# Attention in groups of four heads and one query block, with two-bank exponentials and four banks for scores beside two for maxima

## The reference

```python
def attn(h, Wq, bq, Wk, bk, Wv, bv, Wo, bo):           # 16 heads, hd = 16, S = 2048
    q, k, v = (h @ Wq.T + bq), (h @ Wk.T + bk), (h @ Wv.T + bv)   # each reshaped to (B, S, 16, 16)
    scores = jnp.einsum('bqhd,bkhd->bhqk', q, k) / jnp.sqrt(hd)
    scores = jnp.where(causal, scores, finfo.min)
    attn = jax.nn.softmax(scores, axis=-1)
    return jnp.einsum('bhqk,bkhd->bqhd', attn, v).reshape(B, S, H) @ Wo.T + bo
...
x = x + 0.5 * ffn(layernorm(x))
x = x + attn(layernorm(x))
x = x + 0.5 * ffn(layernorm(x))
```

## Time and profile before

| | |
|---|---|
| median of 3 runs | 1116.4 us (1113.87 to 1118.17) |
| the profiled execution | 1118.69 us, its span 1117.0 us |
| TensorE busy | 1071.8 us (96%) |
| VectorE busy | 699.0 us (63%) |
| ScalarE busy | 577.9 us (52%) |
| GpSimd busy | 112.6 us (10%) |
| mean granted TensorE clock | 0.994 of full speed |
| chain that ended last | PE 87%, DVE 6%, ACT 2%, issue 2%, DMA 1% |

### The profile page before, as it was taken

One profiled execution on the slowest core, in us unless ns is written; L12 is line 12 of the kernel. 1 busy time (PEld: TensorE's weight loads), 2 busy tenths in 40 slices (PEclk: granted clock), 3 DMA queues, 4 the chain that ended last, 5 costly groups with the idle time before them and its releaser, 6 DMA issues.

```text
span 1117.0 us, 17563 instructions
## 1 busy us (share of the span) xinstructions
PE 1071.8 (96%) x6448; PEld 707.1 (63%) x6448; DVE 699.0 (63%) x1620; ACT 577.9 (52%) x1107; POOL 112.6 (10%) x409
## 2 busy tenths in 40 slices
PE   4999999998999989999999999999999999999998
PEld 3888888887876533333333333333349888888887
DVE  5986545446556487888888888888544434344333
ACT  4764443342344656666777776777663333333322
POOL 1000000000001136331111111111100000000000
PEclk9999999998999899999999999999999999999999
DMA  6001040060030732322022202200000000000000
GB/s 195 2 1 47 7 126 1 11 175 16 10 123 1 202 65 55 67 53 53 14 41 54 53 1 54 53 1 2 1 1 1 1 20 1 1 19 1 20 1 19
DMA packets 75223, 43.81 MB, mean 39 GB/s; under 512 B 47161, under 2 KB 68993, under 8 KB 75137
## 3 DMA queue, kind: packets, MB, share of 16 engines
q1 hardware_dynamic: 75137, 42.68, 15.7%
HBM read 25.63 MB, written 16.78 MB: 38 GB/s over the span
## 4 chain that ended last, share of the span: by engine, by line
PE 87%; DVE 6%; ACT 2%; issue 2%; DMA 1%; SPq 0%; POOL 0%; ACTq 0%; DVEq 0%; POOLq 0%
PE psum L850 16%; PE psum L635 14%; PE psum L782 12%; PE psum L723 11%; PE psum L738 10%; PE psum L867 8%; PE psum L650 8%; DVE attn_part_max L1327 2%; PE psum L792 2%; PE psum L682 2%; ACT attn_prob L1141 1%; PE psum L826 1%; PE psum L694 1%; PE psum L124 1%; DVE attn_junk L1330 1%
## 5 line engine op out<-in xcount | busy, mean ns | idle before, releaser
L1141 ACT ACTIVATE attn_prob<-psum 128x512 f32<-128x512 f32 (+3 forms) x640 | 301.2, 540 | 145.7 <-PE psum L723 142.0
L1327 DVE TENSOR_REDUCE attn_part_max<-psum 128x1 f32<-128x512 f32 x384 | 243.7, 684 | 50.1 <-PE psum L738 48.2
L635 PE MATMUL psum<-ffn_xt,all_w_hi 128*128 128x512 f32 x512 | 166.0, 406 | 0.0
L782 PE MATMUL psum<-attn_prob,attn_vals 128*32 128x512 f32 (+3 forms) x1280 | 156.9, 544 | 0.1
L1330 DVE CUSTOM_DVE_ANT_0 attn_junk<-psum,attn_mask 128x128 bf16<-128x128 f32 (+3 forms) x256 | 116.9, 485 | 24.9 <-PE psum L738 24.4
L1432 DVE TENSOR_TENSOR ffn_act_out<-ffn_act_out,psum 128x512 f32<-128x512 f32 x64 | 44.0, 688 | 109.3 <-ACT ffn_act_out L1177 109.2
L650 PE MATMUL psum<-all_w_hi,ffn_inner 128*128 128x256 f32 x512 | 105.0, 288 | 0.1
L1177 ACT ACTIVATE ffn_act_out<-psum 128x512 f32<-128x512 f32 x64 | 38.2, 597 | 127.3 <-PE psum L850 127.3
L635 PEld LDWEIGHTS psum<-ffn_xt,all_w_hi 128*128 128x128 f32 x512 | 92.7, 192 | 16.4 <-issue 0.3
L867 PE MATMUL psum<-all_w_hi,ffn_inner 128*128 128x256 f32 x512 | 102.5, 283 | 0.1
L635 PE MATMUL psum<-ffn_xt,all_w_lo 128*128 128x512 f32 x256 | 100.7, 393 | 0.0
(11 more groups left out here) (150 smaller groups left out, 1674.2 us busy)
## 6 DMA issues: line engine op xcount, KB each, us to landing
qk_rows<-qkv_parts SPq DMA_DIRECT2D x16, 384.0 KB, 2.5
qk_rows<-qkv_parts SPq DMA_DIRECT2D x16, 256.0 KB, 2.9
attn_q_early<-qk_rows SPq DMA_DIRECT2D x8, 384.0 KB, 4.5
attn_q_late<-qk_rows SPq DMA_DIRECT2D x8, 384.0 KB, 3.7
attn_k_mid<-qk_rows SPq DMA_DIRECT2D x3, 768.0 KB, 6.7
attn_k_late<-qk_rows SPq DMA_DIRECT2D x3, 768.0 KB, 7.3
all_x<-in_L_attn_h SPq DMA_DIRECT2D x4, 512.0 KB, 6.7
v_rows<-qkv_rows_v SPq DMA_DIRECT2D x16, 128.0 KB, 2.5
```

Source lines behind the costliest of these rows:

```text
L635: last = nc.tensor.matmul(psum[:, 2 * m + q % 2, :], w_part[a][:, 3 * g + m, pl, o:o + P], xt[:, b % 2, c, pl, :], start=(n == 0), stop=(n ...
L782: last = nc.tensor.matmul(psum[r:r + 32, O0, at:BT], vals[:, k0 * SUB + kb + k, 2 * hd:2 * hd + 32], prob[:, (4 * d + 2 * k + hd) % PRING, ...
L1141: nc.scalar.activation(prob[:, n % PRING, at:BT], psum[:, S0 + n % SBANKS, at:BT], ACT.Exp).then_inc(s["exp"], 1)
L1327: nc.vector.tensor_reduce(to, psum[:, bank, :], AX.X, ALU.max).then_inc(s["max_read"], 1)
```

## The change

Groups become one query block and four heads: 16 groups. A step becomes one block of 128 keys and the four heads' scores, so there are again 160 steps of four scores, 640 maxima and four `weigh` matmuls per step.

- Scores get four banks (2 to 5) and their wait stands on j = 0 and j = 2 alone; one exponential reads two banks and writes 1024 elements (two heads). Maxima get two banks (0 and 1).
- `quota(d)` counts chunks of four maxima: 4 in step 9, 2 in steps 10 to 13, 1.25 a step until step 44, then 1. The chunks of a group are ordered with the key block outermost. Chunks also wait for keys and queries that are loaded four steps before them, so steps 66, 67, 94, 95, 122 and 123 hold none and steps 68, 96 and 124 hold three.
- `turn_max(g)`, `copy_max(g)` and `split_max(g)` run once for four heads, `max_row(g)` issues four DMAs instead of two. By the table, groups 3, 9, 11, 13 and 15 are turned in steps 15, 59, 87, 115 and 143, one step before they begin (16, 60, 88, 116, 144); group 2 is turned in 11 and begins in 12.
- `gather` becomes four transposes of 128 columns per group of four heads. It was four matmuls against a matrix `pick` of 34 columns per group of two heads, which also added the two halves of the sums.
- `mask_prob` clears two heads at once. Keys, queries and values are loaded by query block and by key block, into a ring of six.
- Weight turning and the first output projection move forward by one to three steps.

```diff
-KSLOTS = 12
-LOADS = 3
-SBANKS = 3
-MBANKS = 3
+KSLOTS = 6
+NHQ = 4
+SBANKS = 4
+MBANKS = 2
 PRING = 8
-VW = 34
+VW = 67
+VALUES_AT = (0, 2, 33, 35)
...
-            groups = [(qt, p) for half in range(2) for p in range(NPAIR) for qt in (2 * half, 2 * half + 1)]
+            groups = [(qt, u) for half in range(2) for u in range(NH // NHQ) for qt in (2 * half, 2 * half + 1)]
             NG_A = len(groups)
-            steps = [(g, kb) for g, (qt, _) in enumerate(groups) for kb in range(0, SUB * (qt + 1), 2)]
+            steps = [(g, kb) for g, (qt, _) in enumerate(groups) for kb in range(SUB * (qt + 1))]
...
+            def keys_free(r):
+
+                if r < KSLOTS:
+                    return 8
+                n, c = loads[r - KSLOTS]
+                return begin[2 * n + 1] + SUB * (c + 1)
...
-                return 0 if d < 9 else 4 * (d - 8) if d < 12 else 12 + (d - 11) * 84 // 36 if d < 48 else 96 + 2 * (d - 47)
+                return 0 if d < 9 else 2 * d - 14 if d < 14 else 12 + (d - 13) * 5 // 4 if d < 45 else d + 7
...
-            turn_at = [-2, -2, -2, 1] + [chunk_at[ends[g]] + 2 for g in range(EARLY, NG_A)]
+            turn_at = [-2, 1] + [chunk_at[ends[g]] + 2 for g in range(EARLY, NG_A)]
...
-            S0, M0, O0, X0 = 3, 0, 6, 7
+            S0, M0, O0, X0 = 2, 0, 6, 7
...
                         def max_row(g):
                             sp.wait_ge(s["max_rows"], g + 1)
-                            b, o = g // 2 % QSLOTS, g % 2 * BT
-                            for hd in range(2):
-                                sp.dma_start(queries(b)[KR:KR + NPART, hd, o:o + BT], max_rows[NPART * SUB * hd:NPART * SUB * (hd + 1), g % 2, :]
+                            for hd in range(NHQ):
+                                sp.dma_start(queries(g)[KR:KR + NPART, hd, :], max_rows[NPART * SUB * hd:NPART * SUB * (hd + 1), g % 2, :]
...
-            masks = [(d, j) for d, (g, kb) in enumerate(steps) if kb >= SUB * groups[g][0] for j in range(4)]
+            masks = [(d, j) for d, (g, kb) in enumerate(steps) if kb >= SUB * groups[g][0] for j in (0, 2)]
...
-                            if n >= SBANKS:
-                                pe.wait_ge(s["exp"], n - SBANKS + 1)
+                            if n >= SBANKS and j % 2 == 0:
+                                pe.wait_ge(s["exp"], n - SBANKS + 2)
...
-                            for hd in range(2):
-                                for k in range(2):
-                                    at = first_query(qt, kb + k)
-                                    r = 32 * (2 * hd + k)
-                                    last = nc.tensor.matmul(psum[r:r + 32, O0, at:BT],
-                                                            vals[:, k0 * SUB + kb + k, 2 * hd:2 * hd + 32],
-                                                            prob[:, (4 * d + 2 * k + hd) % PRING, at:BT], start=(kb == 0),
-                                                            stop=(kb == SUB * (qt + 1) - 2), skip_group_check=True)
+                            for hd in range(NHQ):
+                                last = nc.tensor.matmul(psum[32 * hd:32 * hd + 32, O0, at:BT],
+                                                        vals[:, r % KSLOTS * SUB + kb % SUB, VALUES_AT[hd]:VALUES_AT[hd] + 32],
+                                                        prob[:, (4 * d + hd) % PRING, at:BT], start=(kb == 0),
+                                                        stop=(kb == SUB * (qt + 1) - 1), skip_group_check=True)
...
-                                last = nc.tensor.matmul(psum[:, X0, i * VW:(i + 1) * VW], o_sb[:, g % 2, i * P:(i + 1) * P], pick[:, :],
-                                                        start=True, stop=True)
+                                last = nc.tensor.transpose(psum[:, X0, i * P:(i + 1) * P], o_sb[:, g % 2, i * P:(i + 1) * P], ident[:, :])
...
-                                act.wait_ge(s["scored"], n + 1)
-                                nc.scalar.activation(prob[:, n % PRING, at:BT], psum[:, S0 + n % SBANKS, at:BT],
-                                                     ACT.Exp).then_inc(s["exp"], 1)
+                                if j % 2 == 0:
+                                    act.wait_ge(s["scored"], n + 2)
+                                    bank = S0 + n % SBANKS
+                                    nc.scalar.activation(prob[:, n % PRING:n % PRING + 2, at:BT], psum[:, bank:bank + 2, at:BT],
+                                                         ACT.Exp).then_inc(s["exp"], 2)
```

261 lines of the change are left out of this document (124 added, 137 removed).

## The result

The changed kernel takes 1206.2 us (median; 1202.3 to 1208.4) where the one before took 1117.3 in the same runs: ratio 1.0788, 95% interval 1.0738 to 1.0839, 7.9% slower. The direction was forecast (0.91 for slower). The time was not: 1173 predicted, range 1146 to 1195. The profiled execution has a span of 1204.8 us and a mean granted clock of 0.955; before it was 1117.0 and 0.994.

What follows compares the result with a forecast made beforehand. Attention was taken as bound by TensorE's own stream. 1116.4 + 50 (35 for steps 48 to 159, 12 for steps 12 to 47, 3 for steps 0 to 11) + 7 for the clock = 1173 us, range 1146 to 1195.

Steps and rivals of the forecast that it cites:

- Two banks for maxima: In full steps, the third and fourth maximum wait for VectorE's reads: 3.29 us a step, +0.45.
- The rival that gaps absorb half of it: Bank wait's +0.45 us a step shrinks by up to half: +25 instead of +50, 1141 to 1147 us; chance 0.12.
- Steps with several short chunks: In each 28-step cycle, the step with three short chunks (twelve reads) was put at 3.6 us.
- A cycle of 28 steps: Second half of attention: 28 steps take 90.7 us against 2 x 39.25 = 78.5; steps 48 to 159 come to +35.
- Steps 0 to 11: Start of attention: eight more maxima than before at about 0.42 us a read, +3 us.
- my own formula for bodies: First to fourth maximum of a chunk on two banks: 0.42 + 0.60 + 0.68 + 0.06 = 1.76 us; less for short chunks.
- Rows of maxima: TensorE idles 2.6 us at groups 3, 9, 11, 13 and 15, 13 us in all; group 2 is covered.
- The clock: TensorE's clock falls behind two of the five row waits, 3.4 us each: +7 us, ends 0 and +17.
- What is saved: Less TensorE work, inside the sums: gathers 18 us, narrower diagonal `weigh`s 6.4, half as many `turn_max` 2.6.
- the rival "faster, 1102": Reads of maxima don't bind, 1.76 us falls to 1.31 and only the savings stand: 1102 us; chance 0.05.
- Costed at nothing: Paired exponentials (1.03 us for 1024 columns), masks on GpSimd and smaller loads were given no cost.
- Steps 12 to 47: Middle stage of attention, 46 chunks in 36 steps: 126.6 us against 114.2, +12.

Runs made afterwards that it cites:

- the fillers: Changed kernel with 13 extra matmuls of 512 columns ahead of the row waits at groups 3, 9, 11, 13 and 15: 1193.2 us, ratio 1.0668.
- the run made to take these falls away: Changed kernel with the fillers and further extra matmuls in the steps with maxima: 1200.5 us, ratio 1.0726.

## Why the prediction was right in kind and too low

*Two banks for maxima*, the term that decides: right. Full steps 3.31 us (3.29 predicted), the waits on the third and fourth maximum, VectorE idle 0.82 us a step. As a whole, taking the price of the bank apart from the other terms, the prediction had 50 - 13 + 27 = 64 us; the runs show 66.5 (with one DMA) and 69 (in the kernel before). The 69 holds some falls of the clock that I had not placed there (62 in the one execution that had next to none). The rival that gaps absorb half of it is out.

*Steps with several short chunks*: the sum was too low, for two reasons. The 3.6 us are the bodies of three single chunks (0.9 + 1.2 + 1.5), without the stretches between one chunk's last maximum and the next one's first. And I let reads follow each other without a gap. Timeline of the changed kernel in distance 66, with twelve reads of the diagonal:

```profile
616.32 0.29 DVE L1322 CUSTOM_DVE_ANT_0 attn_junk<-psum,attn_mask 128x128 bf16<-128x128 f32 x1 [5.02 <-PE psum L732]
...
616.54 0.29 DVE L1322 CUSTOM_DVE_ANT_0 attn_junk<-psum,attn_mask 128x128 bf16<-128x128 f32 x1
...
617.06 0.29 DVE L1322 CUSTOM_DVE_ANT_0 attn_junk<-psum,attn_mask 128x128 bf16<-128x128 f32 x1 [0.22 <-PE psum L732]
...
617.85 0.42 DVE L1322 CUSTOM_DVE_ANT_0 attn_junk<-psum,attn_mask 128x256 bf16<-128x256 f32 x1 [0.21 <-PE psum L732]
```

Two reads go, then VectorE is idle 0.2 us until the next two banks are filled: a round trip of two reads takes 0.74 to 0.79 us for 128 columns, where two reads take 0.51. Reads of 512 columns follow each other every 0.60 us without such a gap: a long read hides the refill of the other bank, a short one does not. The distance is 6.38 us against 3.6 + 0.22 + 1.31 = 5.1 by my sum, and in two of the three cycles the clock falls behind it (+1.1 and +1.4 us on the next distance). Windows there, in the third cycle:

```profile
809.00:813.00 4.00, 2.74 (x13) 0.81 (x11) 3.39 (x17) 2.05 (x2) 0.00 (x0) 1.00 0.00 0
813.00:817.00 4.00, 4.00 (x16) 0.86 (x15) 1.67 (x7) 0.65 (x1) 0.00 (x0) 0.57 0.22 66
```

*A cycle of 28 steps*: 90.7 predicted; first score to first score of groups 9, 11 and 13 it took 96.3 and 97.0. The 5.6 to 6.3 us are 3.7 to 4.0 for the fall behind the row wait, 1.3 for the short chunks, 0 and 1.1 for the fall behind them and 0.2 for a longer row wait. The sum itself has two gathers at 0.8, where its own 0.48 each make 1.0; it matters little.

*Steps 0 to 11*, "+3": wrong by 10 us. I priced the eight added maxima and forgot that the bank wait holds there too. Distances 7 to 9, with sixteen, eight and eight maxima, take 11.4, 6.9 and 6.9 us, 25.1 in all; before they took 14.3, with three banks 18.4. So the added maxima cost about 4 and the banks about 7. By my own formula for bodies these steps would have come to some 22; I put the rest down to the low clock (0.77 in the stage), which no run shows by itself.

*Rows of maxima*: right. 15.3 us idle in the five places named, group 2 nearly covered (its load waits 0.81 us).

*The clock*, "two of five, +7": the step that failed. Its price for one fall, 3.4 us, was near (4.0, 3.7, 2.6, 2.5 and 0.0 us). The number was not: all five row waits had one, 12.9 us together, and TensorE ran 110 us at 1.2 GHz in all, not two stretches. Falls that the term left out cost as much again. Behind a pair of chunks in step 33, distances 32 to 34 are 4.0 us longer than with the fillers; distance 44 is 1.2 longer than with one DMA; behind the short chunks it is 1.1 and 1.4; and distances 10 to 12, through which a fall from the stage before lasts, are 4.5 over my formula. That is 12 us from the distances, and 17 by the other way: the 59 us at the lower level that the fillers leave over the kernel before, at 0.29 us each. Both are estimates, since the run made to take these falls away cost as much as it gave. Of the 30 us by which the rows of the account exceed the prediction, some 18 are this term's (12.9 and 12 against 7), 10 the first twelve steps', 4 the three steps with short chunks and 2 the longer row waits, less the 4.9 us by which scores began earlier.

The trace before had a warning that I overlooked. I wrote that the clock was 1.00 in the windows of attention and that a wait of 2.6 us is "on the edge". But in steps 0 to 11 the window has 0.93, and there the clock fell for 6.8 us behind two waits of only 1.09 and 0.85 us:

```profile
379.95 0.23 PE L723 MATMUL psum<-attn_q_early,attn_k_early 99*128 99x128 bf16 x1 [0.85 <-ACT attn_prob L1141]
...
376.00:380.00 4.00, 2.07 (x20) 1.35 (x20) 2.08 (x3) 3.69 (x9) 0.90 (x3) 1.00 0.94 288
380.00:384.00 4.00, 4.00 (x21) 2.45 (x21) 1.10 (x3) 2.70 (x7) 1.28 (x4) 0.64 1.15 313
```

The Trainium skill, "TensorE: Matmul & The Clock Gate", section "A second HAM failure mode: psum-queue depth-cycling", says of a measured kernel that cycling through PSUM banks makes it idle in small pieces often enough that the clock swings. Half of this is seen: full steps, with 0.47 us lost to the bank waits in each, stayed at 1.00 through the last stage of 359 us in the old kernel with two banks, but steps of short chunks, with TensorE busy 2.74 of 4 us, were followed by falls in two cycles of three.

*What is saved*, 27 us: right for TensorE's own work, wrong for the time. A gather and the score behind it, in the kernel before and with three banks and one DMA:

```profile
534.52 0.97 PE L792 MATMUL psum<-attn_pick,attn_o_sb 128*128 128x34 f32 x8
535.33 0.38 PE L723 MATMUL psum<-attn_q_early,attn_k_mid 99*128 99x512 bf16 x1
...
597.09 0.60 PE L781 MATMUL psum<-all_ident,attn_o_sb 128*128 128x128 f32 x4
597.52 0.38 PE L714 MATMUL psum<-attn_q_late,attn_k_early 99*128 99x512 bf16 x1
```

It held the score 0.81 us and holds it 0.43 now (0.48 predicted). The step around it was only 0.39 longer than a full one, 3.23 against 2.84, because its `weigh` is of 128 and 256 columns and holds 0.56 where a full one holds 1.00. Yet 28 steps take 78.6 us with three banks and one DMA, and took 78.5 before. What TensorE saves it waits elsewhere, some 5 us in 28 steps (an estimate, from distances less TensorE's own sum of the step; 27 us in 160 steps are 4.7 in 28): 2.6 in two empty steps, which ScalarE holds at 2.46 each, and the one with three short chunks behind them, which together take 9.8; 1.1 in the row wait that one DMA leaves; and 1.7 in steps of narrow scores or narrow maxima, which by TensorE alone would end sooner. Distance 73, for one, takes 2.39 where TensorE's own sum is 1.97, and four reads at 0.60 are 2.40. Steps 0 to 11 hold eight more maxima besides. So the rival "faster, 1102" was not reached with three banks either: 1119.4, and 1115.7 with the short chunks spread.

*Costed at nothing*: nothing of what was named there showed up on the path; a paired exponential took 1.02 us (1.03 predicted).

*Steps 12 to 47* took 13.7 us more than predicted. The clock is most of it: 2.5 behind the row wait of group 3, 4.0 in distances 32 to 34, 1.2 in distance 44 and, as far as the clock explains them, the 4.5 in distances 10 to 12. The row wait itself was 0.6 longer than predicted.

*Open*: scores begin 2.2 to 5.3 us earlier than before in every kernel with groups of four heads. This goes along with a fall of the clock near 268 us, in the first feed-forward layer: 6.8 us long in the three traces with groups of two heads, 3.4 us or absent in the others. No run was made on why.

## What to carry to other kernels

Count banks by the round trip: a ring needs enough of them that a bank's matmul, its reader's start and its read (here 0.42 + 0.68 + 0.06 us for one read, 1.76 for the fourth maximum on two banks) end before the producer comes round to it, and check that for the short reads too, where nothing hides the refill. In an in-order queue what waits behind a full ring is everything: the bank taken away cost 63 to 69 us here, and nothing saved elsewhere paid for it. Look for the falls of the clock in every stage of the trace before, with the waits ahead of them, and price a wait of TensorE as the wait and a fall that may follow. Count a saving on the engine that sets the pace step by step: in a step that another engine already holds it is worth nothing. And when two steps are compared for the cost of one operation, see that they are alike in the rest; a gather seems to cost 0.39 us until one sees the narrow `weigh` beside it.

## What the runs showed of the hardware

Row waits of 2.8 to 3.7 us went with a fall to 1.2 GHz in five cases of five. Shorter ones were mixed: in the changed kernel with one DMA there was a fall at 1.00, 1.41 and 1.85 us and none at 0.94 and 1.02; with three banks and one DMA there was one at 1.63 and 2.52 and none at 1.03, 1.09, 1.26 and 1.42. Full steps with 0.47 us of bank waits each stayed at 2.4 GHz through 359 us. A fall cost 0.0 to 4.0 us. Time at 1.2 GHz cost 0.29 us per us, where TensorE also waits for reads. An issue of rows on SyncE's queue took 0.73 us, and four of them 2.95, one behind the other, though each moves only a few rows.
